# Loading the first half of x tile by tile, with the first weight piece and the constants on ACT's queue

## The reference

```python
# block 1: four experts per batch row, weights are ctx (256x256 each), one expert picked per token by its id
xn = layernorm(x)
for e in range(4):
    g = silu(xn @ ctx[e].T);  u = xn @ ctx[e].T
    y = (g * u) @ ctx[e].T
    out = where(expert_id == e, y, out)
x = x + out
# block 2: 16 routed experts (hidden 96, top 4 by sigmoid score + bias) and one shared expert
xn = layernorm(x)
x = x + sum_e combine[:, e] * (silu(xn @ G_e.T) * (xn @ U_e.T)) @ D_e.T + shared(xn)
```

## Time and profile before

| | us |
|---|---|
| median of 3 runs | 192.96 (191.62 to 195.4) |
| the profiled execution's own time | 193.0 |
| its span, first to last instruction | 190.5 |

### The profile page before, as it was taken

How to read it: one execution, slowest core, us unless ns; L and a number is a source line. 1 busy time by engine, 2 the same in 40 slices (tenths; PEclk the granted TensorE clock), 3 DMA queues, 4 the chain that set the end, 5 groups by cost and what they waited for, 6 DMA issues and landing times.

```text
span 190.5 us, 2267 instructions
## 1 busy us (share of the span) xinstructions
PE 177.9 (93%) x776; PEld 138.3 (73%) x776; DVE 112.5 (59%) x228; ACT 68.3 (36%) x108; POOL 39.6 (21%) x38
## 2 busy tenths in 40 slices
PE   7899999999999759999879999969999999999992
PEld 2478878878878538888667777847888878788761
DVE  1598997865964863478883433763562554445443
ACT  2634234431257237342651527241231223322310
POOL 3792022663200054109950000000000000000000
PEclk9999999999999999999978999999999999999999
DMA  5996012374000012300000000000020000000003
GB/s 146 309 389 239 3 22 90 110 204 126 0 3 0 0 15 97 110 3 2 0 0 3 0 0 0 0 0 3 0 110 0 0 0 3 0 0 0 0 2 110
DMA packets 3866, 10.00 MB, mean 53 GB/s; under 512 B 560, under 2 KB 1168, under 8 KB 3728
## 3 DMA queue, kind: packets, MB, share of 16 engines
q1 hardware_dynamic: 3856, 9.87, 15.9%
HBM read 8.82 MB, written 1.05 MB: 52 GB/s over the span
## 4 chain that ended last, share of the span: by engine, by line
PE 75%; DVE 13%; issue 4%; ACT 4%; DMA 2%; DVEq 0%
PE bank L832 24%; PE bank L915 10%; PE bank L913 9%; PE bank L914 9%; PE bank L933 5%; PE bank L936 5%; PE bank L934 5%; DVE prod L681 3%; DVE hid L694 3%; ACT h_hi L480 2%; PE bank L877 2%; DMA x<-x_d 2%; PE bank L794 1%; DVE stats L555 1%; PE bank L859 1%
## 5 line engine op out<-in xcount | busy, mean ns | idle before, releaser
L915 PE MATMUL bank<-xn_lo,gu_hi 128*128 128x512 f32 (+1 forms) x104 | 41.3, 397 | 0.0
L913 PE MATMUL bank<-xn_hi,gu_lo 128*128 128x512 f32 x96 | 38.3, 399 | 0.0
L914 PE MATMUL bank<-xn_hi,gu_hi 128*128 128x512 f32 x96 | 38.1, 397 | 0.0
L681 DVE TENSOR_TENSOR prod<-act_sb,bank 128x512 f32<-128x512 f32 x24 | 16.5, 686 | 33.3 <-PE bank L877 30.5
L480 ACT ACTIVATE h_hi<-hid 128x512 fp32r<-128x512 f32 (+1 forms) x26 | 16.4, 631 | 52.6 <-DVE hid L694 52.6
L699 DVE TENSOR_TENSOR h_lo<-hid,h_hi 128x512 fp32r<-128x512 f32 (+1 forms) x26 | 20.2, 778 | 21.9 <-ACT h_hi L480 21.9
L915 PEld LDWEIGHTS bank<-xn_lo,gu_hi 128*128 128x128 f32 (+1 forms) x104 | 19.5, 188 | 5.0
L470 ACT ACTIVATE act_sb<-bank 128x512 f32<-128x512 f32 (+1 forms) x26 | 15.4, 594 | 18.9 <-PE bank L915 18.8
L913 PEld LDWEIGHTS bank<-xn_hi,gu_lo 128*128 128x128 f32 x96 | 18.3, 191 | 4.5
L914 PEld LDWEIGHTS bank<-xn_hi,gu_hi 128*128 128x128 f32 x96 | 18.3, 190 | 4.4
L933 PE MATMUL bank<-h_hi,wd_lo 128*128 128x512 f32 (+1 forms) x52 | 21.2, 409 | 0.1
(11 more groups left out here) (82 smaller groups left out, 223.7 us busy)
## 6 DMA issues: line engine op xcount, KB each, us to landing
stage<-gu_d SPq DMA_DIRECT2D x6, 512.0 KB, 3.5
stage<-wd_d SPq DMA_DIRECT2D x3, 512.0 KB, 3.5
stage<-ctx_d SPq DMA_DIRECT2D x4, 256.0 KB, 5.2
xt<-xt_d SPq DMA_DIRECT2D x1, 1024.0 KB, 9.4
out_d<-xt SPq DMA_DIRECT2D x3, 256.0 KB, 2.2
x<-x_d SPq DMA_DIRECT2D x2, 256.0 KB, 3.6
x<-x_d SPq DMA_DIRECT2D x1, 512.0 KB, 6.6
ids<-ids_d SPq DMA_DIRECT2D x1, 512.0 KB, 7.4
```

The costliest lines, as they stand in the source:

```text
L681: nc.vector.tensor_tensor(prod[:, g % 2], act_sb[:, g % 2], side_bank("spread", *items[g])[:], ALU.mult).then_inc(prod_done, 1)
L913: nc.tensor.matmul(out[:], gu_lo[:, cols], xn_hi[:, h, k], start=(k == 0), stop=False)
L914: nc.tensor.matmul(out[:], gu_hi[:, cols], xn_hi[:, h, k], start=False, stop=False)
L915: ins = nc.tensor.matmul(out[0:rows, :], gu_hi[:, wide], xn_lo[:, h, k], start=False, stop=(k == KC - 1))
```

## The change

The first half of x is loaded as four transfers of one tile each, each with its own semaphore, and DVE waits for one tile at a time. Piece 0 and the constants are issued by ACT, as its first two instructions, and SP's queue goes from x tile 3 on to piece 1. `BY_VECTOR[0]` becomes (0, 2, 3), so DVE normalises tile 3 too, and ACT only tile 1; ACT's call for the second pair, which also waited for the second `shift`, is gone. Counts of semaphores follow the new split.

```diff
-BY_VECTOR = ((0, 2), (0, 2), (0, 1), (0, 2))
+BY_VECTOR = ((0, 2, 3), (0, 2), (0, 1), (0, 2))
-        x_in = [sem(f"x_in{n}") for n in range(3)]
+        x_in = [sem(f"x_in{n}") for n in range(TT + 1)]
...
             mine = t in BY_VECTOR[n]
             before = sum((u in BY_VECTOR[n]) == mine for u in range(t))
-            eng.wait_ge(normed_v if mine else normed_a, n * TT // 2 + before + 1)
+            earlier = sum((u in BY_VECTOR[m]) == mine for m in range(n) for u in range(TT))
+            eng.wait_ge(normed_v if mine else normed_a, earlier + before + 1)
...
-            sp.dma_start(x[:, 0:TT // 2], x_d[:, 0:TT // 2]).then_inc(x_in[0], 16)
-            sp.dma_start(x[:, TT // 2:TT], x_d[:, TT // 2:TT]).then_inc(x_in[1], 16)
-            load_piece(0)
-            sp.dma_start(consts_sb[:], consts_d).then_inc(consts_in, 16)
+            for t in range(TT):
+                sp.dma_start(x[:, t], x_d[:, t]).then_inc(x_in[t], 16)
             for n in range(1, SLOTS):
                 load_piece(n)
-            sp.dma_start(x[:, TT:], x_d[:, TT:]).then_inc(x_in[2], 16)
+            sp.dma_start(x[:, TT:], x_d[:, TT:]).then_inc(x_in[TT], 16)
...
+            dram, st, _, _ = piece_aps(0)
+            nc.scalar.dma_start(st, dram).then_inc(slot_in[0], 16)
+            nc.scalar.dma_start(consts_sb[:], consts_d).then_inc(consts_in, 16)
             nc.scalar.preload_act_table(ACT.Silu)
             apply_norm(0, range(TT // 2))
             high_part(0)
-            apply_norm(0, range(TT // 2, TT))
             high_part(1)
...
-            for n, tiles in enumerate((range(TT // 2), range(TT // 2, TT))):
-                dve.wait_ge(x_in[n], 16)
+            for tiles in (range(TT // 2), range(TT // 2, TT)):
                 for t in tiles:
+                    dve.wait_ge(x_in[t], 16)
                     tile_stats(0, t)
                 layer_norm_vars(0, tiles)
```

More of the change, by code:

```diff
@@ L221, in wait_ring_read @@
             elif what == "x1":
-                eng.wait_ge(normed_v, (HALVES + 1) * TT // 2)
-                eng.wait_ge(normed_a, (HALVES + 1) * TT // 2)
+                eng.wait_ge(normed_v, sum(len(BY_VECTOR[m]) for m in range(HALVES + 1)))
+                eng.wait_ge(normed_a, sum(TT - len(BY_VECTOR[m]) for m in range(HALVES + 1)))
         def side_bank(what, h, c):
@@ L447, in copy_x1 @@
             def copy_x1(h):
-                act.wait_ge(normed_v, HALVES * TT // 2)
+                act.wait_ge(normed_v, sum(len(BY_VECTOR[m]) for m in range(HALVES)))
                 for pair in range(KC):
@@ L716, in _ @@
             x_low("n1", 0, 1)
-            dve.wait_ge(x_in[2], 16)
+            dve.wait_ge(x_in[TT], 16)
             for t in range(TT):
```

## The result

| | before | changed |
|---|---|---|
| median | 192.81 us (191.62 to 195.4, 6 runs) | 195.3 us (194.26 to 196.04, 6 runs) |
| profiled execution, its span | 193.0, 190.5 us | 194.26, 192.3 us |
| time outside that span | 2.5 us | 1.96 us |

The ratio is 1.014, with a 95% interval of 1.009 to 1.019. A second set of six runs of the changed kernel gave 195.51 us and 1.017 (1.012 to 1.021). The kernel became slower, as forecast, but by 2.5 us where 1.1 were forecast; within 2% it stayed, as forecast too. The ratios leave out runs that stand over 1.5% above the fastest of their kernel, which takes from the kernel before its runs of 195 us and from the changed kernel none, so they lean against the changed kernel: over all runs the first ratio is 1.011 in place of 1.014.

A forecast was written before the change was run, and what follows sets the result against it. The prediction took PE to bound the kernel, so the start of `mix(0)` sets the end. Tile 3 on DVE added about nothing, x's later landing 1.1 us: 194.1 us from a median of 192.96, range 192.2 to 195.3 us.

The forecast's parts named there:

- What bounds the kernel: PE, busy 93% of the span; any shift of the start of `mix(0)` in the head moves the end equally.
- The queue's part: In the head, piece 0 and constants on ACT's queue take DMA time from x's tiles 2 and 3: 1.1 us later.
- L: The time at which x's tile 3 lands in the head: taken as 6.7 us, with break-even at 5.6 us.
- rival (b): ACT's queue fills idle engine time in the head; tile 3 lands at 5.6 to 6.2 us; costs 0 to 0.6 us; chance 0.17.
- the range of the forecast: Tile 3 lands in the head at 6.2 to 7.3 us, costing 0.6 to 1.7 us, 194.1 us; chance 0.55.
- Two such tiles in a row take DVE 0.73 us: In the head, DVE's normalisation of tiles 2 and 3 would end at 8.21 us, against 8.19 us on ACT.
- part one: DVE normalises tile 3 in the head: worth about nothing, a gain of at most 0.6 us.
- The sum: `x_high` and `mix(0)` in the head start 1.1 us later, `mix(0)` at 10.55 us; total 194.1 us.
- Rival (d), the clock: PE idles some 2 us before `mix(0)` and the granted clock falls: +1.1 + 1.3 us, 195.4 us; chance 0.06.
- Rivals (a): SP's queue served first or ACT's transfers late; tiles 2 and 3 land by 5.25 us; gain 0.3 to 0.6 us; chance 0.22.

The follow-up runs named there:

- the loads alone: The changed kernel with tile 3 normalised by ACT again, the loads left as changed: 192.95 us against 192.84, ratio 1.003.
- the filled one: Loads as changed, tile 3 on ACT, with products of zeros in PE's waits of block 2: 191.39 us.
- block 2 filled: The changed kernel with products of zeros on PE in three of its waits of block 2: 194.38 us, and 192.96 us on another chip.
- a head filled alone: The changed kernel with three products of zeros on PE before its wait for tile 3 and three before `mix(0)`: 195.33 us.
- the run with tiles on SP: The kernel before with x's first half in four one-tile transfers, everything else on SP behind them, tile 3 on ACT: ratio 1.001.

## Why the prediction was wrong in size and right in sign

- **What bounds the kernel, and that the start of `mix(0)` sets the end**: right for the span. 1.49 us in the head became 1.8 us at the end. Of the other 0.3 us, 0.36 stand as issue time before the last group's product on DVE, whose cause is open. It goes with tile 3 on DVE: that change alone moved the head by 0.97 and the span by 1.3 us, the loads alone moved them by 0.48 and 0.5 us. What the prediction took as fixed, the 2.5 us outside the span, shrank to 1.96 us.
- **The queue's part**: right in mechanism, too large in size. L was taken as 6.7 us. In the first profile and in five others with these loads it was about 6.1 us, in the range of rival (b), and in four more 6.4 to 7.0 us, in the range of the forecast. The term 6.7 + 0.37 - 5.94 = 1.1 us measured 0.61 us in the first profile. The price of the part was 0.5 us in the first profile of the loads alone and 0.8 us (10.28 against 9.45 us) in the filled one.
- **"Two such tiles in a row take DVE 0.73 us"**: this is the step that failed, the term of part one. It measured 1.68 us. The earlier trace rows are from 15.51 us, where POOL ended its instruction at 15.57 us, as DVE began. In the head POOL starts its first low part 0.2 us after DVE's tile 2, so tile 3 would meet it. The trace of before even had a case that the prediction left unused: two normalisations at 90 us, beside POOL's low parts.

```profile
90.03 2.78 DVE L578 TENSOR_SCALAR xn<-x,meanvar,rstd 128x256 f32<-128x256 f32 x2
```

- **The sum**: +1.1 us came near the head's 1.49 us, and near the 1.3 us between the two profiled executions, by luck: the queue's term was 0.5 us too large, that of DVE 0.97 us too small, and of two that it did not have one added 0.3 us at the end and one took off 0.5 us outside the span.
- **Rival (d), the clock**: right as a mechanism, wrong in its chance, and this is the second step that failed. Taken at 0.06 with a price of 1.3 us, it happened in 5 and in 11 of 12 runs of the changed kernel with block 2 filled and costs 1.5 us. The argument against it counted the warm-up but not that DVE's wait for POOL would leave PE idle for another 0.8 us. The median has 2.5 us where the profiled executions have 1.3: more frequent falls (three of six runs at 0.98, twice) and later landings of x. How much of that is the head's is open. Kernels without the filling mix falls in both places, a head filled alone changed nothing, and the two profiled executions of the changed kernel fell in block 2 only.
- **Rivals (a) and (b)**: SP's queue was not served first; tile 1 landed 0.9 us later than the first pair had. Of (b), the time of the loads alone came true (+0.1 us of median, ratio 1.003), but not for its reason, as the span shows.

## What to carry to other kernels

Work moved to DVE must be priced by a row of the same instruction in which POOL is as busy as it will be there: the normalisation took 0.41 us or 1.36 us, the statistics were not held. A change of the span is not yet one of the time: here 0.5 to 0.6 us went missing between the two, so both must be compared. Transfers that are issued ahead of others on a second queue take their time from the first, so put there only what is needed first. Idle time of PE costs more than itself when the granted clock falls behind it, and cheap products of zeros in PE's own waits can buy that back: on this kernel 0.6% (191.38 us against 192.97), and by 191.98 against 192.92 us on another chip, 0.3% (0.994 to 1.000). That filled kernel, and the filled one with x in tiles on SP (191.38 us, ratio 0.988, 0.982 to 0.993, on a chip where the kernel before had a median of 193.51 us), beat both kernels; between these two no difference was measured, and the filled kernel with the changed loads and tile 3 on ACT (191.39 us) was no slower.

## What was not expected of the hardware

The landing of the same small transfer varies between executions: the statistics of tile 3, with the same loads, began between 6.1 and 7.04 us. And 20 warm-up products ended anywhere from 7.15 us (1.31 + 5.84) to 8.76 us (1.31 + 7.45), by when their pace went from 0.43 to about 0.2 us; in the late cases they, and not x, held the transposes, as `mix(0)` at 10.05 us in the run with tiles on SP shows. The unchanged head alone started `mix(0)` at 9.45, 9.52 and 10.31 us in three profiled executions. A head that is tuned to 0.3 us is below this spread. The time outside the span, 2.4 us or 1.8 to 1.95 us by version and steady within each, was not expected either.
